# Score passes in pairs on the two row halves of the tensor array, in an attention and mixture-of-experts kernel

## The reference

```python
# attention: 16 heads of width 8, window of 64 keys
q, k, v = split(layernorm(x) @ Wqkv);  q, k = rope(q, k)
scores  = q @ k.T / sqrt(8), where 0 <= i - j < 64, else -inf
x = x + (softmax(scores) @ v) @ Wout
# feed-forward on xf = layernorm(x)
shared  = (silu(xf @ sg) * (xf @ su)) @ sd
# router: best 4 of 8 groups, then best 4 of 32 experts; gates = softmax of the 4 scores
# each expert takes its first `capacity` tokens in token order (a running count per expert)
h = silu(buf @ wg) * (buf @ wu);  out_e = h @ wd
x = x + shared + sum over the 4 experts of gate * out_e
```

## Time and profile before

| | us |
|---|---|
| three timed executions | 888.08, 897.61, 899.48 |
| median | 897.61 |
| the profiled execution, first to last instruction | 904.6 |

### The profile page before, as it was taken

One profiled execution on the slowest core, in us unless ns is written; L12 is line 12 of the kernel. 1 busy time (PEld: TensorE's weight loads), 2 busy tenths in 40 slices (PEclk: granted clock), 3 DMA queues, 4 the chain that ended last, 5 costly groups with the idle time before them and its releaser, 6 DMA issues.

```text
span 904.6 us, 24570 instructions
## 1 busy us (share of the span) xinstructions
PE 724.0 (80%) x7521; PEld 563.5 (62%) x7521; DVE 534.0 (59%) x2192; ACT 360.9 (40%) x853; POOL 415.1 (46%) x548
## 2 busy tenths in 40 slices
PE   3798888988978788898888858888888888877960
PEld 1565656665646565575665637777777777777540
DVE  3476756556577676656666656545454454543598
ACT  4465544454455445444454423332323232322200
POOL 4125343353343434334344350555555555556555
PEclk9698776676798878767788859999999999998985
DMA  8991000000000000000000002423233333421355
GB/s 268 358 390 35 14 20 15 12 23 12 12 22 10 20 9 15 10 7 14 6 7 6 6 8 84 125 76 105 76 114 107 114 115 103 126 75 32 122 182 167
DMA packets 52338, 68.37 MB, mean 76 GB/s; under 512 B 9505, under 2 KB 31807, under 8 KB 52304
## 3 DMA queue, kind: packets, MB, share of 16 engines
q1 hardware_dynamic: 38240, 53.56, 18.4%
q0 software_dynamic: 9216, 11.97, 4.4%
q10 hardware_dynamic: 4848, 2.40, 0.9%
HBM read 34.89 MB, written 39.99 MB: 83 GB/s over the span
## 4 chain that ended last, share of the span: by engine, by line
PE 52%; another core or an unknown queue 19%; issue 10%; DVE 10%; ACT 6%; POOL 1%; ACTq 1%; DVEq 1%; POOLq 0%
PE bank L693 9%; PE bank L864 7%; PE bank L680 6%; PE bank L674 5%; PE bank L663 5%; PE bank L657 3%; PE bank L701 3%; DVE x_all L1246 3%; DVE mx L1044 2%; PE bank L733 2%; ACT hact L607 2%; PE bank L817 2%; PE bank L756 1%; PE bank L747 1%
## 5 line engine op out<-in xcount | busy, mean ns | idle before, releaser
L463 POOL DMA_INDIRECT pair_results<-yout,yidx x160 | 157.2, 982 | 143.4 <-ACT yout L625 104.0
L447 POOL DMA_INDIRECT expert_slots<-xfe,sidx x128 | 127.0, 992 | 141.5 <-DVE sidx L1148 108.3
L864 PE MATMUL bank<-xgT_parts,wgu_parts 128*128 128x320 f32 x768 | 147.2, 344 | 46.4 <-ACT hact L607 46.4
L864 PEld LDWEIGHTS bank<-xgT_parts,wgu_parts 128*128 128x128 f32 x768 | 125.9, 208 | 57.3 <-ACT hact L607 50.3
L519 ACT ACTIVATE pt<-bank 128x512 f32<-128x512 f32 x128 | 76.2, 596 | 182.2 <-PE bank L680 164.9
L1259 DVE TENSOR_TENSOR hact<-hact,bank 128x320 f32<-128x320 f32 x128 | 57.1, 481 | 140.2 <-ACT hact L607 133.1
L1044 DVE TENSOR_REDUCE mx<-bank 128x4 f32<-128x512 f32 x128 | 87.3, 683 | 32.5 <-PE bank L663 19.7
L421 POOL TENSOR_TENSOR pout<-pin,mhalf 128x3 f32<-128x3 f32 (+2 forms) x36 | 29.9, 830 | 127.4 <-DVE pin L970 127.4
L890 PE MATMUL bank<-wdn,hact 128*128 128x128 f32 x640 | 82.7, 288 | 2.3 <-issue 2.3
L890 PEld LDWEIGHTS bank<-wdn,hact 128*128 128x128 f32 x640 | 82.5, 207 | 2.5 <-issue 2.5
L623 ACT COPY yout<-bank 128x512 f32<-128x512 f32 x32 | 18.7, 585 | 162.2 <-remote 151.0
(11 more groups left out here) (148 smaller groups left out, 1335.1 us busy)
## 6 DMA issues: line engine op xcount, KB each, us to landing
expert_slots<-fill SPq DMA_DIRECT2D x32, 322.5 KB, 6.5
xg<-expert_slots SPq DMA_DIRECT2D x32, 322.5 KB
pair_results<-rload SPq DMA_DIRECT2D x32, 256.0 KB
rload<-pair_results SPq DMA_DIRECT2D x16, 512.0 KB, 4.0
wgu<-in_L_ffn_wg_dram SPq DMA_DIRECT2D x32, 128.0 KB
wgu<-in_L_ffn_wu_dram SPq DMA_DIRECT2D x32, 128.0 KB
wdn<-in_L_ffn_wd_dram SPq DMA_DIRECT2D x32, 128.0 KB
pair_results<-yout,yidx POOLq DMA_INDIRECT x160
```

The costliest lines, as they stand in the source:

```text
L447: g.indirect_dma_start(out=slots_d, out_offset=bass.IndirectOffsetOnAxis(ap=sidx[:, tr.b, k:k + 1], axis=0), in_=xfe[:, tr.b, k, :], in_of ...
L463: g.indirect_dma_start(out=pairs_d, out_offset=bass.IndirectOffsetOnAxis(ap=yidx[:, c, j:j + 1], axis=0), in_=yout[:, c, j, :], in_offset= ...
L864: last = mm(bank[2 + 2 * w + h][:, 0:CH], wgu_parts[:, e.b, wp, w, h * P:(h + 1) * P], xgT_parts[:, e.b, xp, ch * CH:(ch + 1) * CH], start ...
```

## The change

The four units of a tile become two pairs `w`; a pair is the two units with the same `g4`, one in each row half of the array.

- `first_scores(w)` fills banks 0 and 1 together. The mask becomes four products of 64 rows and 64 columns over 512 columns each, one for each quarter of the array, and the 16 score products go round the four quarters. The pair waits for both maxima of the pair before.
- `second_scores(w)` fills banks 2 and 3 together. The mask is a product of its own (64 rows, 512 columns), one in each row half. The maxima come in through eight products of 64 rows with `pick` as weights and `mT`, the transposed maxima, as moving data; `mT` is laid out so that each row half holds its own heads' parts. The 16 score products alternate between the row halves. The pair waits for both exponentials of the pair before.
- `weighted_values(w)` orders the 16 products of a pair so that consecutive ones go to four different column groups.
- The order on PE changes: the second scores of pair 0 move from behind the first scores to before the router product L725, behind the transposes of k. The others stand as first scores 0, output projection, first scores 1, second scores 1, values 0, running counts, values 1.
- The transpose of `xn` moves from bank 3 to bank 7, the transpose of `on` and the output projection from bank 3 to bank 6, the running counts to other columns of bank 6. The waits change with them: the router product also waits for `xnT_evac`, the transpose of `on` for `kT_evac`, the running counts for `x1_ready`.
- At the start ACT makes one cast `pick` in place of two casts `comb_st`; POOL clears `mp`; a few constants leave the constant table.

The order of the operations on DVE, ACT and POOL stays as it is.

```diff
--- before.py
+++ after.py
...
@@ -142,8 +139,9 @@
         before_b = sb("before_b", [P, P], BF16)
         ones_b = sb("ones_b", [P, P], BF16)
         maskq_b = sb("maskq_b", [P, P], BF16)
-        comb_st = sb("comb_st", [P, H, P], BF16)
-        comb_mv = sb("comb_mv", [P, 2, P], BF16)
+        eye2_b = sb("eye2_b", [P, P], BF16)
+        pick = sb("pick", [P, NG, P], BF16)
+        mT = sb("mT", [P, 2, P], BF16)
         cent = sb("cent", [NGR + NE, D])
         cent_sq = sb("cent_sq", [NGR + NE, D])
         cent_n = sb("cent_n", [NGR + NE, 4])
...
@@ -645,53 +641,69 @@
             pe.wait_ge(S.attn_w_loaded, 16 * 2)
 
             def step(tau, tn, tf, tp, ts, tw, tr):
-                def first_scores(u):
-
-
-                    s, g4 = u % NS, u // NS * 4
-                    bk = bank[u % 2]
-                    wait(pe, S.p1_reduced, NU * tp.n + (u - 1) if not isinstance(tp.n, int) or tp.n else u - 1)
-                    if u == 1:
+                def first_scores(w):
+
+
+                    n, g4 = NU // NS * tp.n + w, 4 * w
+                    wait(pe, S.p1_reduced, NS * n)
+                    if w == 0:
 
                         wait(pe, S.mT_evac, tp.n)
-                    mm(bk[:, :].rearrange("p (c j) -> p c j", c=4), ident_b[:, :],
-                       maskq_b[:, :].unsqueeze(1).broadcast_to([P, 4, P]), start=True, stop=False,
-                       skip_group_check=True)
-                    rows = slice(STRIP * s, STRIP * (s + 1))
-                    for hb in range(2):
-                        for c in range(4):
-                            last = mm(bk[hb * WIN:(hb + 1) * WIN, c * P:(c + 1) * P],
-                                      qT[rows, tp.b, g4 + c, hb * WIN:(hb + 1) * WIN],
-                                      kT[rows, tp.b, g4 + c, hb * WIN:hb * WIN + P], start=False, stop=(c == 3),
-                                      skip_group_check=True)
-                    last.then_inc(S.p1_scores, 1)
-                def second_scores(u):
-
-                    s, g4 = u % NS, u // NS * 4
-                    bk = bank[2 + u % 2]
-                    wait(pe, S.exp_done, NU * ts.n + (u - 1) if not isinstance(ts.n, int) or ts.n else u - 1)
+                    hold(pe)
+                    for s in range(NS):
+                        rows = slice(STRIP * s, STRIP * (s + 1))
+                        for hb in range(2):
+                            mm(bank[s][hb * WIN:(hb + 1) * WIN, :].rearrange("p (c j) -> p c j", c=4),
+                               ident_b[rows, rows], maskq_b[rows, :].unsqueeze(1).broadcast_to([STRIP, 4, P]),
+                               start=True, stop=False, skip_group_check=True)
                     for c in range(4):
-                        mm(bk[:, c * P:(c + 1) * P], comb_st[0:WIN + 3 * H, NS * (g4 + c) + s, :],
-                           comb_mv[0:WIN + 3 * H, ts.b, :], start=(c == 0), stop=False, skip_group_check=True)
-                    rows = slice(STRIP * s, STRIP * (s + 1))
+                        for s in range(NS):
+                            rows = slice(STRIP * s, STRIP * (s + 1))
+                            for hb in range(2):
+                                last = mm(bank[s][hb * WIN:(hb + 1) * WIN, c * P:(c + 1) * P],
+                                          qT[rows, tp.b, g4 + c, hb * WIN:(hb + 1) * WIN],
+                                          kT[rows, tp.b, g4 + c, hb * WIN:hb * WIN + P], start=False, stop=(c == 3),
+                                          skip_group_check=True)
+                            if c == 3:
+                                last.then_inc(S.p1_scores, 1)
+                def second_scores(w):
+
+                    n, g4 = NU // NS * ts.n + w, 4 * w
+                    wait(pe, S.exp_done, NS * n)
+                    hold(pe)
+                    for s in range(NS):
+                        rows = slice(STRIP * s, STRIP * (s + 1))
+                        mm(bank[2 + s][:, :].rearrange("p (c j) -> p c j", c=4), maskq_b[rows, :],
+                           eye2_b[rows, :].unsqueeze(1).broadcast_to([STRIP, 4, P]),
+                           start=True, stop=False, skip_group_check=True)
+                    for c in range(4):
+                        for s in range(NS):
+                            rows = slice(STRIP * s, STRIP * (s + 1))
+                            mm(bank[2 + s][:, c * P:(c + 1) * P], pick[rows, g4 + c, :], mT[rows, ts.b, :],
+                               start=False, stop=False, skip_group_check=True)
                     for c in range(4):
                         for hb in range(2):
-                            at = c * P + hb * WIN
-                            last = mm(bk[:, at:at + WIN], kT[rows, ts.b, g4 + c, hb * WIN:hb * WIN + P],
-                                      qT[rows, ts.b, g4 + c, hb * WIN:(hb + 1) * WIN], start=False,
-                                      stop=(c == 3 and hb == 1), skip_group_check=True)
-                    last.then_inc(S.p2_scores, 1)
-                def weighted_values(u):
-
-                    pe.wait_ge(S.exp_done, NU * ts.n + (u + 1))
-                    for c in range(4):
-                        h = NS * (u // NS * 4 + c) + u % NS
+                            for s in range(NS):
+                                rows = slice(STRIP * s, STRIP * (s + 1))
+                                at = c * P + hb * WIN
+                                last = mm(bank[2 + s][:, at:at + WIN], kT[rows, ts.b, g4 + c, hb * WIN:hb * WIN + P],
+                                          qT[rows, ts.b, g4 + c, hb * WIN:(hb + 1) * WIN], start=False,
+                                          stop=(c == 3 and hb == 1), skip_group_check=True)
+                                if c == 3 and hb == 1:
+                                    last.then_inc(S.p2_scores, 1)
+                def weighted_values(w):
+
+                    pe.wait_ge(S.exp_done, NU * ts.n + NS * (w + 1))
+                    for c in range(0, 4, 2):
                         for hb in range(2):
-                            vals = (v_cur if hb else v_mix)[:, ts.b, h, :]
-                            at = c * P + hb * WIN
-                            to = h // 4 * P + hb * WIN
-                            last = mm(bank[7][32 * (h % 4):32 * (h % 4 + 1), to:to + WIN], vals,
-                                      pt[:, ts.b, u, at:at + WIN], start=True, stop=True)
+                            for cc in (c, c + 1):
+                                for s in range(NS):
+                                    h = NS * (4 * w + cc) + s
+                                    vals = (v_cur if hb else v_mix)[:, ts.b, h, :]
+                                    at = cc * P + hb * WIN
+                                    to = h // 4 * P + hb * WIN
+                                    last = mm(bank[7][32 * (h % 4):32 * (h % 4 + 1), to:to + WIN], vals,
+                                              pt[:, ts.b, NS * w + s, at:at + WIN], start=True, stop=True)
                     return last
                 def transposed_parts(t, w):
                     pe.wait_ge(S.split_hi, 2 * t.n + 2)
@@ -712,16 +724,24 @@
                 if tf is not None:
                     pe.wait_ge(S.xn_ready, tf.n + 1)
 
-                    wait(pe, S.exp_done, NU * (tf.n - 2))
-                    nc.tensor.transpose(bank[3][:, 2 * P:3 * P], xn[:, tf.b], ident[:, :]).then_inc(S.xnT_done, 1)
+                    wait(pe, S.pv_evac, tf.n - 2)
+                    nc.tensor.transpose(bank[7][:, P:2 * P], xn[:, tf.b], ident[:, :]).then_inc(S.xnT_done, 1)
                 if tp is not None:
 
+                    wait(pe, S.x1_ready, tp.n - 2)
                     wait(pe, S.pos_read, tp.n - 3)
                     transposed_parts(tp, 1)
+                if ts is not None:
+                    pe.wait_ge(S.mT_evac, ts.n + 1)
+
+                    wait(pe, S.onorm, ts.n)
+                    second_scores(0)
                 if tr is not None:
                     pe.wait_ge(S.xfT_evac, tr.n + 1)
 
                     pe.wait_ge(S.pv_evac, min(tr.n + 2, NT) if isinstance(tr.n, int) else tr.n + 2)
+                    if tf is not None:
+                        pe.wait_ge(S.xnT_evac, tf.n + 1)
                     mm(bank[7][:, 0:NGR + NE], xfT[:, tr.b], centT[:, :], start=True, stop=True)\
                       .then_inc(S.router_done, 1)
                 if tf is not None:
@@ -736,15 +756,18 @@
                         nc.tensor.transpose(bank[0][:, 0:NGR + NE], cent_sq[:, :], ident[0:NGR + NE, 0:NGR + NE])\
                           .then_inc(S.centT_done, 1)
 
-                        pe.wait_ge(S.fills, 6)
-                        pe.wait_ge(S.comb_cast, 2)
+                        pe.wait_ge(S.fills, 7)
+                        pe.wait_ge(S.comb_cast, 1)
                         pe.wait_ge(S.centT_evac, 1)
                 if tw is not None:
                     pe.wait_ge(S.onorm, tw.n + 1)
```

(51 more changed lines are left out.)

51 lines of the change are left out of this document (25 added, 26 removed).

## The result

| | before | after |
|---|---|---|
| median, same chip | 894.68 us (888.08 to 899.48, 4 runs) | 918.27 us (916.5 to 919.87, 4 runs) |
| ratio, 95% interval | 1 | 1.0286 (1.0205 to 1.0367) |
| profiled execution: own time, span, clock | 904.6 us, 0.829 (span, clock) | 919.87 us, 918.1 us, 0.834 |

A forecast was written before the change was run, and what follows sets the result against it. The bound was taken to be the loop through POOL's DMAs and DVE's order, not PE; a step of 16.07 us becomes 14.4, saving 42 us over 25 steps plus 6 outside, 48 in all: median 897.6 to 850 us, range 818 to 885.

The forecast's parts named there:

- the moved second scores: Second scores of pair 0 ahead of the router product: 0.4 us a step longer, between nothing and 0.9.
- signs of a wrong prediction: Maxima 2 later than R+3.9, L405 over 0.5 us after the DMAs, or a changed wait before maxima 0.
- the rival that makes it go (805 us): DVE's 2.55 us wait before maxima 0 vanishes with shorter PE passes; step 12.3 to 12.6 us; chance 0.10.
- The row halves do work side by side: First pass on PE: row halves wholly parallel, a pair costing what a unit does, 0.66 or 0.99 us.
- A pair of the second pass: Second scores on PE with overlapping row halves: 0.98 us at clock 1.0 or 1.49 at 0.5, from 1.34 or 2.16.
- The wait of L1129 for L794: DVE's wait for the running counts on PE after maxima 3: to shrink from 1.9 us to under 0.3.
- From L404 to the end of sidx: Rotary sum on POOL (L405 before) until slot numbers are ready: 8.3 us at clock 1.0, 8.6 at 0.5, from 10.36.
- R: Start of the rotary sum L405 on POOL; maxima 2 were forecast to start at R+3.44 or R+3.77, from R+3.34.
- 1.3, 0.7 and 0.4: PE time saved per step at clock 1.0 in first pass, second pass and values; summed there as 2.5 us.
- Turns (920 us): Row halves of PE take turns instead of overlapping, so pairs get dearer; 23 us slower; chance 0.09.
- The clock (865 us): PE's clock falls with more idle time; steps of 14.8 to 15.0 us if all ran at 0.5; chance 0.15.
- PE's gain off the path (885 us): Another loop step, such as ACT's exponentials, keeps the running counts late; only 0.4 us a step comes off; chance 0.09.

The follow-up runs named there:

- a_pair0_mid: Changed kernel with the second scores of pair 0 moved between the output projection and the first scores of pair 1: 856.48 us, ratio 0.9599 to the kernel before.
- after_again: The changed kernel, unaltered, run again on another chip of the slower kind: 916.61 us, ratio 1.0281 to the kernel before.
- after_third: The changed kernel, unaltered, on a chip where the kernel before takes about 725 us: 758.85 us, ratio 1.0457.
- b_extra64: Kernel before plus one product of 64 rows ahead of the router product, standing in for the kernel before on a faster chip: 727.37 us beside 726.78.
- a_units_first: Changed kernel, first pass by units as before, second scores of pair 0 behind the output projection: 852.99 us (0.9565); again on a faster chip 738.29 us (1.0199).
- a_no_rows: Changed kernel with every slot number out of bounds, so the indirect DMAs are issued but move no rows: 918.57 us, a single time.

## Why the prediction was wrong

**The step that failed is "the moved second scores".** I took 0.4 us a step, because 0.58 us of idle time and 1.80 us of slack of L405 would hide the block, and gave 0.9 as the upper bound. On 895 chips the block's own time is about what I said (285.61 to 286.52, 0.91 us, nearly all at full clock). But L404 starts 3.16 us later than right behind the DMAs; over 0.5 was one of my own signs of a wrong prediction. Undoing the place alone, a_pair0_mid against after_again on one chip, gives 856.48 against 916.61 us, and the step 14.73 against 16.93: the term of 0.4 us measures 2.2. The slack that I counted ran from the product's end in PE's records to its use. It left out that on this chip a reader can come much later than that end. The trace of before had that in plain sight: "2.55 <-remote" in front of maxima 0.

**I misread that wait.** I tied it to L405 because it ended 0.92 us after L405's start. It ends 5.8 us after the first DMA, wherever L404 or L405 is: 5.82 in the step of the earlier trace rows and in a_pair0_mid. In the kernel after it is L1074 that comes at 5.89. On a 725 chip maxima 0 start 1.8 us ahead of L405 (3.07 against 4.89). So the rival that makes it go (805 us) had its argument against it from a coincidence; and the forecast lacked the rival in which this wait moves from maxima 0 to the router's scores. There DVE's router and rotary work, 2.2 us from L1074 to the start of L404 (289.96 to 292.13), comes to stand behind it instead of ahead of it. That is the result, by the medians of the table: the rotary sum starts 3.0 us later, and from there to the end of the step it takes 2.4 less (8.98 instead of 11.37), so the step is 0.6 longer.

**What was right.** The row halves do work side by side. Sixteen products L663 take the time of the eight before, 0.67 us at clock 0.5 (294.34) and 0.39 to 0.42 at 1.0 on the 725 chip, against 0.65 and 0.42 in the earlier trace rows. The mask alone, estimated at 0.21 us at full clock, takes 0.22 there (L656 to L663 in after_third). A pair of the second pass takes 294.94 to 296.33 = 1.39, for which 1.49 was forecast. "TensorEngine Tiling (Array Packing)" in the Trainium skill, section Key Properties, says that tiles operate independently; the traces now agree. The wait of L1129 for L794 is gone, L1138 starts behind maxima 3 (297.62 - 296.97 = 0.65). From L404 to the end of sidx I forecast 8.3 and got 8.04, but by luck: maxima 2 came at R+2.91 and not at the forecast R+3.44, since maxima 0 no longer waited for R+0.92. The fair comparison is a_pair0_mid, where maxima 0 are at R+0.9 again: there maxima 2 start at R+3.8 and sidx ends at R+9.0, against the 3.4 to 3.8 and the 8.3 to 8.6 of the forecast. The step is 14.73, at the upper end of the forecast's 14.1 to 14.8 though without the 0.4 of the moved block, and the kernel takes 856 us where I said 850. One slip in the sum changes nothing: 1.3, 0.7 and 0.4 make 2.4 us a step off PE, not 2.5.

**The rivals.** Turns (920 us) has the right time for the wrong reason: its mechanism is refuted by the sixteen products. The clock (865 us): 0.77 in the stage against 0.78, no part of it on the 895 chips; on the 725 chips, where the transposes slow down, it is a part of the loss. PE's gain off the path (885 us) had the running counts as late as before; they no longer hold anything, so that is refuted too.

**Why the gain of the halves shows on one kind of chip alone.** On the 895 chip the counts were late, and the halves remove that: maxima 3 to sidx goes from 5.01 to 3.04 us. On the 725 chip it is 3.04 before: in b_extra64 DVE's list of waits between 100 and 372 us does not have this wait at all, so there is nothing to gain behind maxima 3. What is left is the price of the order: a_units_first, with the block behind the output projection, needs 3.49 us there. These 0.45 us are the wait for the running counts come back; in the same stretch of a_units_first_again it makes 11.6 us, in 16 of 22 steps (L1137 behind L802), 0.5 a step. Why the counts are late there, with shorter passes, I have not taken apart; the granted clock is 0.91 against 1.00 in b_extra64.

**Open.** What makes a reader wait on an 895 chip, and why the moved block sets it off. It is not the time of the product against the DMAs alone: in a_units_first it ends 1.75 to 2.1 us after the first DMA in several steps and is read at 2.0 to 2.1; in the kernel after it ends at 1.6 to 3.2 and is read at 5.7 to 5.9. The kernel before has shorter waits of this kind already: its product ends at 2.2 to 2.3 in several steps and is read at 2.8, 3.6 or 4.3. Since PE's own products pause among themselves there (289.02 and 289.74 above), it is not even settled whether the readers see a finished result late or PE finishes it later than the modelled ends of its records say. It is not the bytes (a_no_rows). Whether it is the DMAs' issue or their packets, and whether the number of products or their kind counts, is not decided.

## To carry to other kernels

Work that is moved ahead of a product on which another engine's long chain depends is priced by when the reader starts in the trace, not by the end of the producer's records; where waits put down to "remote" sit at a fixed distance from an event (5.8 us from the first indirect DMA here), ask which reader will stand there after the change. Shorter passes on the busiest engine (92 us less PE time here) are worth what the waits of the loop's other engines give back, so keep the shortening and the reordering apart, and time each by itself. Measure on more than one chip: the best order here was 4.3% faster on one and 2.0% slower on another.
